# Expert blocks whose three layers are spread over three steps, with their weights in three transfers

## The chip, the cores and the metric

The kernel runs on one core of a Trainium2 chip. Its engines are TensorE (PE, with its weight loads as PEld), VectorE (DVE), ScalarE (ACT), GpSimd (POOL) and SyncE (SP); each takes its own instructions in order, and they meet by semaphores. The metric is the time of one execution in microseconds of device time. Before the change it is 2029.61 us, the median of three runs (2027.33 to 2029.68).

## The reference

The input is `x` (6250 nodes x 256, fp32) and 200,000 edges, `src` to `dst`, sorted by `dst`. Two stages follow each other:

```python
x = x + gnn(layernorm(x), edges)      # two layers
x = x + ffn(layernorm(x))             # six experts, two per node

# gnn, each of two layers l, over the edges and one loop per node:
h   = x @ W[l]
agg = segment_sum(norm[:, None] * h[src], dst) + b[l]
x   = relu(agg + x_res @ resW + resb)

# ffn:
rh     = relu(features @ router_w1 + router_b1)             # 256 -> 128
logits = softmax(rh @ router_w2 + router_b2)                # 6 experts
top_w, top_i = top_k(logits, 2); weights = softmax(top_w)
h1 = relu(features @ expert_w1 + b1)                        # 256 -> 256, each expert
h2 = relu(h1 @ expert_w2 + b2)
expert_out = h2 @ expert_w3 + b3
combined = sum over the two chosen experts of weight * expert_out
```

## The kernel before

The graph stages count the edges between tiles of nodes into matrices of fp16 and sum messages by products with them; they fill the time to about 1620 us and the change does not touch them. In the last pass each pair of node tiles (25 pairs, the last of one tile) is also normalised and routed: the router's products, the choice of two experts with their weights (`choices`, `gates`), and the place of each node in its expert's list (`place`), to which GpSimd scatters its row. There are two tables of such rows, one for the first choice and one for the second.

The **expert stage** reads these tables in blocks of 256 rows of one expert, at most 30 blocks for each choice (`NB`), so 60 blocks (`BLOCKS`). Blocks 0 to 29 compute the first choice's part and scatter `x + weight * expert` to a table `first_out`; blocks 30 to 59 compute the second choice's part, gather the rows of `first_out` by token, add to them and scatter to the output. Which expert and which row a block begins with stands in `block_table`. Its first 17 blocks (`EARLY_BLOCKS`) are settled early by `early_list`; the rest by `final_list` (lines 2215 to 2257), a chain of 25 small VectorE instructions, once the last tile has been placed.

The stage has no scheduler: each engine's order is written by hand, as a loop over steps b. TensorE's step was: the second layer of block b, the turn (four transposes) of block b+2, the first layer of block b+1, the output product of block b (`products`, lines 2130 to 2149).

```python
self.second_layer(pe, b, k)
self.turn(pe, b + 2, ...)
self.first_layer(pe, b + 1, ...)
self.outs(pe, b, k)
```

A layer writes two PSUM banks, one for each half of its 256 outputs. ScalarE empties the lower half with bias and relu (`low`, line 2158) and copies the turned rows (`y_copy`, line 2154); VectorE empties the upper half (`high`, line 2261). Per step VectorE also makes the scatter's row numbers (`index`, 2282 and 2284), the sum of bias and rows (`add_bias`, 2265), the normalised rows of block b+3 in the first choice (`normal`, 2289), and the result (`add_outs`, 2273). The last pair's routing is spread over the first steps by functions called `beside(b)`, on each engine.

SyncE loads weights and rows (`loads`, 2062 to 2077): after the result of block b it reads the expert from `block_table` (a `value_load`), loads the weights of block b+3 as one transfer into one of three slots (`load_weights`, 2042 to 2044), and then the rows of block b+6 (`load_rows`, 2047 to 2049). GpSimd scatters each block (2346) and, for the second choice, gathers the rows of block b+2 ahead of it (2339); the gather begins when all of the first choice has been stored.

## Time and profile before

| what | value |
|---|---|
| runs | 2027.33, 2029.61, 2029.68 us |
| profiled execution, span | 2027.2 us |
| expert stage, second layer of block 0 to outs of block 59 | 1622.15 to 2012.31 us |
| TensorE busy, whole span | 1845.7 us (91%) |
| VectorE, ScalarE, GpSimd busy | 1120.7, 771.5, 387.4 us |
| DMA, whole span | 208 GB/s of HBM traffic |
| weights | 60 transfers of 898.0 KB |
| rows | 60 transfers of 260.0 or 258.0 KB |

The page gives no other time of the profiled execution than its span, which lies 0.1 us below the fastest run and 2.4 us below the median. TensorE is busy for most of the span, but a stage can still wait: the busy share is an average over stages with different limits, and matmul ends are modelled. So the expert stage is read by itself, in stretches.

### The profile page before, as it was taken

The numbers are of one execution on the slowest core, as the hardware profiler recorded it, in microseconds if no ns is written. First come the engines' busy times: TensorE is split into PE (matmuls) and PEld (weight loads), VectorE is DVE, ScalarE is ACT, GpSimd is POOL, SyncE is SP. The second block draws the span as 40 slices with busy tenths as digits, with TensorE's granted clock in tenths as the row PEclk, the third lists the DMA queues.
The fourth block names the chain that finished last, engine by engine and source line by source line (L and its number), as shares of the span: only waits on it lengthen the run. The fifth ranks groups of instructions, "written<-read, shape, count | busy, mean of one in ns | idle before, by whom it ended". The sixth has DMA issues, their size and how long they took to land. (4 is left out here: it accounts for less than half of the span.)

```text
span 2027.2 us, 34554 instructions
## 1 busy us (share of the span) xinstructions
PE 1845.7 (91%) x11170; PEld 1128.0 (56%) x11170; DVE 1120.7 (55%) x2788; ACT 771.5 (38%) x1686; POOL 387.4 (19%) x403
## 2 busy tenths in 40 slices
PE   4448799999999999999959999999999988998886
PEld 3336555555555555555524445444454476886775
DVE  7246766666666666666504444444444566644443
ACT  2226755665566655665501222222222232221221
POOL 1680000000000000000000211111211133335664
PEclk8769899999999999999979999999999999998998
DMA  6255399998999972323364555444555556767783
GB/s 221 58 85 111 106 330 308 285 333 257 293 293 272 282 248 94 153 108 134 154 274 159 184 193 203 173 174 170 184 202 196 186 183 200 253 214 234 256 254 123
DMA packets 121920, 412.55 MB, mean 204 GB/s; under 512 B 14633, under 2 KB 75009, under 8 KB 115577
## 3 DMA queue, kind: packets, MB, share of 16 engines
q1 hardware_dynamic: 82936, 283.65, 40.2%
q0 software_dynamic: 37904, 124.85, 21.9%
q10 hardware_dynamic: 1008, 3.21, 0.4%
q8 instruction: 32, 0.52, 0.1%
q14 instruction: 40, 0.32, 0.1%
HBM read 201.60 MB, written 219.99 MB: 208 GB/s over the span
## 5 line engine op out<-in xcount | busy, mean ns | idle before, releaser
L1383 PE MATMUL bank<-parts,counts 128*128 128x512 f16 x2401 | 643.3, 378 | 0.0
L1383 PE MATMUL bank<-parts,counts_again 128*128 128x512 f16 x2401 | 540.3, 381 | 18.5 <-DMA counts_again<-counts_table 18.5
L1547 ACT ACTIVATE counts<-bank 128x392 f16<-128x392 f32 x800 | 395.1, 497 | 311.2 <-PE bank L1463 304.5
L1383 PEld LDWEIGHTS bank<-parts,counts_again 128*128 128x128 f16 x2401 | 234.1, 99 | 288.4 <-issue 17.0
L594 DVE TENSOR_TENSOR rows_lo<-pair_keys,iota_lo 128x2048 bf16<-128x2048 bf16 x200 | 244.9, 1225 | 239.4 <-PE bank L1463 239.3
L1463 PEld LDWEIGHTS bank<-rows_hi,rows_lo 128*128 128x128 bf16 x3200 | 227.6, 99 | 203.7 <-issue 27.1
L1463 PE MATMUL bank<-rows_hi,rows_lo 128*128 128x98 bf16 x3200 | 277.8, 210 | 11.3 <-DVE rows_hi L594 10.5
L1383 PEld LDWEIGHTS bank<-parts,counts 128*128 128x128 f16 x2401 | 192.5, 96 | 103.6 <-issue 1.1
L454 POOL DMA_INDIRECT first_rows<-route_rows,route_spot_i x49 | 47.9, 977 | 825.7 <-DVE tokens L445 817.7
L594 DVE TENSOR_TENSOR rows_hi<-pair_keys,iota_hi 128x1568 bf16<-128x1568 bf16 x200 | 193.5, 967 | 0.0
L2261 DVE TENSOR_SCALAR h_t<-bank,counts_again 128x256 f32<-128x256 f32 x120 | 57.7, 483 | 161.4 <-PE bank L2097 115.6
L2158 ACT ACTIVATE h_t<-bank,counts_again 128x256 f32<-128x256 f32 x120 | 56.9, 474 | 206.9 <-PE bank L2097 161.5
L2118 PE MATMUL bank<-counts_again,h_t 128*128 128x256 f32 x480 | 116.3, 386 | 10.5 <-issue 7.3
L2097 PE MATMUL bank<-h_t,counts_again 128*128 128x256 f32 x480 | 116.0, 385 | 9.7 <-DVE h_t L2261 5.7
L2097 PE MATMUL bank<-y_t,counts_again 128*128 128x256 f32 x480 | 116.8, 387 | 8.8 <-DMA counts_again<-expert_pack 5.0
L911 PE MATMUL bank<-both_w,feat 128*128 128x256 f32 x196 | 65.3, 465 | 60.8 <-issue 34.5
L1399 ACT ACTIVATE middle<-bank 128x256 f32<-128x256 f32 x98 | 37.3, 381 | 214.8 <-PE bank L1383 214.8
L2118 PEld LDWEIGHTS bank<-counts_again,h_t 128*128 128x128 f32 x480 | 92.2, 193 | 25.3 <-issue 11.6
L2097 PEld LDWEIGHTS bank<-h_t,counts_again 128*128 128x128 f32 x480 | 91.6, 193 | 25.0 <-ACT h_t L2158 9.3
L2097 PEld LDWEIGHTS bank<-y_t,counts_again 128*128 128x128 f32 x480 | 87.6, 192 | 22.2 <-DMA counts_again<-expert_pack 7.5
L375 DVE TENSOR_TENSOR route_prob<-bank,router_b_sb 128x12 f32<-128x12 f32 (+1 forms) x25 | 4.2, 170 | 162.4 <-PE bank L365 162.4
L183 PE MATMUL bank<-both_w,x_t 128*128 128x512 f32 x196 | 93.6, 600 | 0.5 <-ACT x_t L173 0.5
(259 smaller groups left out, 1843.1 us busy)
## 6 DMA issues: line engine op xcount, KB each, us to landing
counts_table<-counts SPq DMA_DIRECT2D x25, 3136.0 KB, 13.7
counts_again<-counts_table SPq DMA_DIRECT2D x24, 3136.0 KB, 11.4
counts_again<-expert_pack SPq DMA_DIRECT2D x60, 898.0 KB
first_rows<-zero_rows POOLq DMA_DIRECT2D x3, 10530.0 KB, 58.4
second_rows<-zero_rows POOLq DMA_DIRECT2D x3, 10449.0 KB, 70.2
res_tile<-res_table SPq DMA_DIRECT2D x98, 128.0 KB, 6.5
first_rows<-zero_rows POOLq DMA_DIRECT2D x1, 10270.0 KB, 61.8
second_rows<-zero_rows POOLq DMA_DIRECT2D x1, 10191.0 KB, 66.7
```

The costliest lines, as they stand in the source:

```text
L183: mm = nc.tensor.matmul(self.product_bank[:, :], self.x1_t[:, o, k * P:(k + 1) * P], self.both_w[:, self.l + 1, k, :], start=k == 0, stop= ...
L454: pool.indirect_dma_start(table, bass.IndirectOffsetOnAxis(ap=self.spot_i[:, b, c, o:o + 1], axis=0), rows[:, b, o, lo:hi], None, bounds_c ...
L594: return nc.vector.tensor_tensor(rows, k, v, ALU.is_equal)
L911: mm = nc.tensor.matmul(res_bank(t)[:, 0:dim], feat[:, t, k * P:(k + 1) * P], both_w[:, 0, k, dim:2 * dim], start=k == 0, stop=k == K2 - 1)
L1383: mm = nc.tensor.matmul(acc[:, 0:2 * dim], lhs, rhs, start=s == 0, stop=s == tiles)
L1399: nc.scalar.activation(middle[:, o, :], bank[half_bank + o][:, dim:2 * dim], ACT.Copy, scale=1.0 / LOW).then_inc(middle_out, 1)
L1463: mm = nc.tensor.matmul(bank[4 + q % 4][:, u * width:(u + 1) * width], rows_lo[:, r % 2, at, :, u % 2], rows_hi[:, r % 2, at, :, u % 2], s ...
L1547: nc.scalar.activation(counts[:, b, :, :].rearrange("p s (o n) -> p o s n", o=2)[:, :, :, q * QUAD:(q + 1) * QUAD], bank[4 + q % 4][:, 0:Q ...
L2097: mm = nc.tensor.matmul(to[m][:, 0:ROWS], weights_of(k, n)[:, kf, m * P:(m + 1) * P], source[:, k % 2, kf, :], start=kf == 0, stop=kf == K ...
L2118: mm = nc.tensor.matmul(outs_bank[k % 2][:, cols_of], h2_t[:, k % 2, kf, h * P:(h + 1) * P], weights_of(k, 2)[:, kf, :], start=kf == 0, st ...
L2158: nc.scalar.activation(to[:, k % 2, 0, :], frm[0][:, 0:ROWS], ACT.Relu, bias=bias_of(k, n, 0)).then_inc(low_out, 1)
L2261: nc.vector.tensor_scalar(to[:, k % 2, 1, :], frm[1][:, 0:ROWS], bias_of(k, n, 1), 0.0, ALU.add, ALU.max).then_inc(high_out, 1)
```

## The change

**The order.** A step on TensorE is now: the first layer of block b+2, the turn of block b+3, the second layer of block b+1, the output product of block b. Before the loop stand the first layer of block 1, the turn of block 2 and the second layer of block 0. ScalarE and VectorE follow in the same order. On VectorE the upper half of the first layer of b+2 comes first; then come the piece of routing or list, the row numbers, the bias sum, the normalised rows (now of block b+4), the upper half of the second layer of b+1, and the result. Each layer also waits until the halves of the block before it are emptied, since its bank is written while an older block is still on its way.

**The weights.** A block's weights are packed as three parts, each a layer's matrix with its bias (514, 514 and 768 columns), and loaded as three transfers with a semaphore each: a part is asked for as soon as its layer of the slot's former block has been emptied.

**The list.** `final_list` is cut into `blocks_held` (step 9), `final_list` (step 10) and `block_ends` (step 11). The routing pieces of the last pairs move by a step in places.

**A semaphore.** In `gather_sum`, five semaphores become one, `column_made`. That function belongs to the path for graphs that the counting path can't take.

```diff
+    W_AT = (0, K2 * dim + K2, 2 * (K2 * dim + K2), W_COLS)
...
-                def load_weights(self, sp, b, k):
-                    e = sp.value_load(block_table[0:1, 0, bass.ds(b, 1)], min_val=0, max_val=experts - 1)
-                    sp.dma_start(w[:, k % WB, :], expert_pack[bass.ds(e, 1), :, :].rearrange("a p n -> p (a n)")).then_inc(w_loaded[k % WB], 16)
+                def expert_of(self, sp, b):
+                    return sp.value_load(block_table[0:1, 0, bass.ds(b, 1)], min_val=0, max_val=experts - 1)
+
+                def load_weights(self, sp, e, k, n):
+                    part = slice(W_AT[n], W_AT[n + 1])
+                    sp.dma_start(w[:, k % WB, part], expert_pack[bass.ds(e, 1), :, part].rearrange("a p n -> p (a n)")).then_inc(w_loaded[n][k % WB], 16)
...
                 def early_weights(self, sp):
-                    for b in range(WB):
-                        self.load_weights(sp, b, b)
+                    for b, n in ((0, 0), (1, 0), (0, 1), (2, 0), (1, 1), (0, 2), (2, 1), (1, 2), (2, 2)):
+                        self.load_weights(sp, self.expert_of(sp, b), b, n)
+
+                def first_weights(self, sp, b, k):
+                    e = self.expert_of(sp, b + WB)
+                    sp.wait_ge(h1_low_out, b + 1)
+                    sp.wait_ge(h1_high_out, b + 1)
+                    self.load_weights(sp, e, k, 0)
...
                         def body(b, k):
+                            if not (isinstance(b, int) and b + 2 + WB >= BLOCKS):
+                                self.first_weights(sp, b + 2, k + 2)
+                            if not (isinstance(b, int) and b + 1 + WB >= BLOCKS):
+                                self.second_weights(sp, b + 1, k + 1)
...
+                            e = self.expert_of(sp, b + WB)
                             sp.wait_ge(result_ready, b + 1)
-                            self.load_weights(sp, b + WB, k)
+                            self.load_weights(sp, e, k, 2)
+                            if isinstance(b, int) and b + SB == EARLY_BLOCKS:
+                                sp.wait_ge(list_ready, 2)
+                                router.wait_scattered(sp, pairs)
                             if first is not None:
                                 self.load_rows(sp, b + SB, k, first)
...
                 def first_layer(self, pe, b, k, r):
-                    pe.wait_ge(w_loaded[k % WB], r * (16 * SB // WB) + 16 * (k // WB + 1))
+                    pe.wait_ge(w_loaded[0][k % WB], weights_count(r, k))
                     pe.wait_ge(y_out, b + 1)
+                    if not (isinstance(b, int) and b < 1):
+                        pe.wait_ge(h1_low_out, b)
+                        pe.wait_ge(h1_high_out, b)
...
                             b = r * SB + k
+                            if not (last and k + 2 >= SB):
+                                self.first_layer(pe, b + 2, *ahead(r, k, 2))
+                            if not (last and k + 3 >= SB):
+                                self.turn(pe, b + 3, *ahead(r, k, 3), second)
+                            if not (last and k + 1 >= SB):
+                                self.second_layer(pe, b + 1, *ahead(r, k, 1))
                             if isinstance(b, int) and b < 2 * SB:
                                 beside(b)
-                            self.second_layer(pe, b, k)
-                            if not (last and k + 2 >= SB):
-                                self.turn(pe, b + 2, (k + 2) % SB, r + (k + 2) // SB, second)
-                            if not (last and k + 1 >= SB):
-                                self.first_layer(pe, b + 1, (k + 1) % SB, r + (k + 1) // SB)
-                            self.outs(pe, b, k)
+                            self.outs(pe, b, k, r)
...
                             if c:
                                 dve.wait_ge(first_back[k % 3], (r - NB // SB) * (32 * SB // 3) + 32 * (k // 3 + 1))
-                            self.add_bias(dve, b, k, c)
+                            self.add_bias(dve, b, k, r, c)
+                            if not c and not (isinstance(b, int) and b + 4 >= NB):
+                                self.normal(dve, b + 4, k + 4, r + (k + 4) // SB)
+                            if not (last and k + 1 >= SB):
+                                second(b + 1, (k + 1) % SB)
                             if not (start and k < 2):
                                 dve.wait_ge(result_stored[k % 2], r * (16 * SB) + 32 * (k // 2))
-                            if not c and not (isinstance(b, int) and b + 3 >= NB):
-                                self.normal(dve, b + 3, k + 3, r + (k + 3) // SB)
                             self.add_outs(dve, b, k, c)
...
-                        if b == 8:
+                        if b == 7:
                             router.count_before(pe, LAST_PAIR, 1)
```

TensorE, before, from the second layer of block 0 on. `y_t` marks a first layer, `h_t` as second input a second layer, `ident` a turn, `counts_again,h_t` the outs (`counts_again` is the buffer that holds the weights); L415 and L416 count the router's choices.

```order
L2097 MATMUL bank<-h_t,counts_again 128x256 x4
L2091 MATMUL bank<-ident,rows 128x128 x4
L2097 MATMUL bank<-y_t,counts_again 128x256 x4
L2118 MATMUL bank<-counts_again,h_t 128x256 x4
L415 MATMUL bank<-route_pick,upper_b 128x24
L416 MATMUL bank<-route_pick,ones_b 128x24
L2097 MATMUL bank<-h_t,counts_again 128x256 x4
L2091 MATMUL bank<-ident,rows 128x128 x4
L2097 MATMUL bank<-y_t,counts_again 128x256 x4
L2118 MATMUL bank<-counts_again,h_t 128x256 x4
L2097 MATMUL bank<-h_t,counts_again 128x256 x4
```

In each step the two layers stand on either side of the turn, and the outs follow the first layer.

The same engine now, from the second layer of block 0 on.

```order
L2126 MATMUL bank<-h_t,counts_again 128x256 x4
L2126 MATMUL bank<-y_t,counts_again 128x256 x4
L2120 MATMUL bank<-ident,rows 128x128 x4
L2126 MATMUL bank<-h_t,counts_again 128x256 x4
L2155 MATMUL bank<-counts_again,h_t 128x256 x4
L2126 MATMUL bank<-y_t,counts_again 128x256 x4
L2120 MATMUL bank<-ident,rows 128x128 x4
L2126 MATMUL bank<-h_t,counts_again 128x256 x4
L415 MATMUL bank<-route_pick,upper_b 128x24
L416 MATMUL bank<-route_pick,ones_b 128x24
L2155 MATMUL bank<-counts_again,h_t 128x256 x4
```

First layer, turn, second layer and outs now belong to four different blocks, and the count of choices stands between a second layer and the outs of the block before.

VectorE, before, at the end of the list in step 9 (L2251 to L2257) and the rest of that step.

```order
L2251 TENSOR_TENSOR more_held<-placed_to 128x2x5
L2252 TENSOR_SCALAR more_held<-placed_to 128x2
L2253 TENSOR_TENSOR weighed<-past,more_held 128x360
L2254 TENSOR_REDUCE block_end<-weighed 128x60
L2256 TENSOR_TENSOR block_end<-block_end,placed_to 128x60
L2257 TENSOR_TENSOR ends<-block_end,block_row 128x43
L2282 TENSOR_SCALAR unused<-row_of,ends 128x2
L2284 TENSOR_TENSOR to_token<-rows,unused 128x2
L2265 SCALAR_TENSOR_TENSOR both_w<-counts_again,rows 128x256 x2
L2289 TENSOR_SCALAR rows<-rows 128x256 x2
L2273 SCALAR_TENSOR_TENSOR both_w<-bank,rows,both_w 128x256 x2
L2261 TENSOR_SCALAR h_t<-bank,counts_again 128x256 x2
```

Both upper halves (`h_t`) stand together, after the result (L2273), and the list stands ahead of all of the step's other work.

The same engine now, in step 11, from the upper half of the first layer of block 13 on, with the last part of the list (L2310 to L2316).

```order
L2320 TENSOR_SCALAR h_t<-bank,counts_again 128x256
L2310 TENSOR_TENSOR more_held<-placed_to 128x2x5
L2311 TENSOR_SCALAR more_held<-placed_to 128x2
L2312 TENSOR_TENSOR weighed<-past,more_held 128x360
L2313 TENSOR_REDUCE block_end<-weighed 128x60
L2315 TENSOR_TENSOR block_end<-block_end,placed_to 128x60
L2316 TENSOR_TENSOR ends<-block_end,block_row 128x43
L2342 TENSOR_SCALAR unused<-row_of,ends 128x2
L2344 TENSOR_TENSOR to_token<-rows,unused 128x2
L2325 SCALAR_TENSOR_TENSOR both_w<-counts_again,rows 128x256 x2
L2349 TENSOR_SCALAR rows<-rows 128x256 x2
L2320 TENSOR_SCALAR h_t<-bank,counts_again 128x256
```

The two upper halves are apart: the second layer's comes after the bias sum (L2325) and the normalised rows (L2349), and the result after it.

## Rows read from the trace of the kernel before

**Rows 1.** Stretches of the expert stage: us, busy us per engine (instructions), TensorE clock, DMA.

```profile
1622.15:1704.20 82.05, 67.23 (x319) 56.44 (x320) 55.28 (x200) 21.39 (x43) 25.61 (x26) 0.96 0.58 181
1704.20:1818.08 113.88, 113.05 (x561) 99.10 (x560) 67.59 (x193) 30.91 (x60) 38.88 (x40) 1.00 0.75 243
1818.08:1830.73 12.65, 7.39 (x30) 5.95 (x29) 3.63 (x10) 1.54 (x3) 7.54 (x8) 0.80 0.36 110
1830.73:1939.43 108.70, 95.34 (x450) 80.18 (x449) 45.97 (x125) 24.41 (x48) 66.74 (x65) 0.98 0.78 251
1939.43:1996.81 57.38, 52.28 (x251) 44.67 (x252) 27.40 (x76) 13.91 (x27) 36.73 (x36) 1.00 0.79 252
1996.81:2012.31 15.50, 14.87 (x70) 12.47 (x68) 8.02 (x20) 2.97 (x6) 10.14 (x10) 1.00 0.24 83
```

**Rows 2.** Timeline, TensorE, one step: start, us, line, out<-in, count [idle before <-releaser].

```profile
1760.74 1.89 PE L2097 MATMUL bank<-h_t,counts_again 128*128 128x256 f32 x8
...
1762.47 0.60 PE L2091 MATMUL bank<-ident,rows 128*128 128x128 f32 x4
...
1762.91 1.89 PE L2097 MATMUL bank<-y_t,counts_again 128*128 128x256 f32 x8
...
1764.63 1.89 PE L2118 MATMUL bank<-counts_again,h_t 128*128 128x256 f32 x8
...
1766.36 1.89 PE L2097 MATMUL bank<-h_t,counts_again 128*128 128x256 f32 x8
```

**Rows 3.** Waits of TensorE, 1622 to 1704 us: total, times, longest.

```profile
PE bank L2091 <- DVE rows L2289: 9.7, 3, 6.4
PE bank L415 <- DVEq L403: 3.4, 2, 1.8
```

**Rows 4.** Timeline, VectorE: first and last of the 25 list instructions.

```profile
1688.95 0.16 DVE L2229 TENSOR_TENSOR held_i<-placed_to,region_base 128x12 int32<-128x12 f32 x1
...
1696.20 0.20 DVE L2257 TENSOR_TENSOR ends<-block_end,block_row 128x43 f32<-128x43 f32 x1
```

**Rows 5.** The chain of work that ended last: start, us, what.

```profile
1935.09 7.46 DMA counts_again<-expert_pack
```

**Rows 6.** Timeline, all engines, around the turn to the second choice.

```profile
1812.98 0.88 DVE L2273 SCALAR_TENSOR_TENSOR both_w<-bank,rows,both_w 128x256 f32<-128x256 f32 x2 [0.22 <-PE bank L2118]
...
1814.68 0.33 SPq L2044 DMA_DIRECT2D counts_again<-expert_pack  x1
...
1821.05 1.07 POOL L2339 DMA_INDIRECT rows<-first_out,to_token  x1 [4.09 <-issue]
...
1825.27 0.88 DVE L2265 SCALAR_TENSOR_TENSOR both_w<-counts_again,rows 128x256 f32<-128x256 f32 x2 [7.68 <-DMA rows<-first_out,to_token]
...
1827.61 3.75 PE L2118 MATMUL bank<-counts_again,h_t 128*128 128x256 f32 x8 [5.26 <-issue]
```

**Rows 7.** Timeline, VectorE and TensorE, a step of the second choice.

```profile
1908.09 1.89 PE L2097 MATMUL bank<-y_t,counts_again 128*128 128x256 f32 x8
...
1912.93 0.48 DVE L2261 TENSOR_SCALAR h_t<-bank,counts_again 128x256 f32<-128x256 f32 x1 [4.49 <-remote]
...
1913.56 1.97 PE L2097 MATMUL bank<-h_t,counts_again 128*128 128x256 f32 x8 [1.85 <-DVE h_t L2261]
```

**Rows 8.** Timeline, SyncE: three weight loads issued in a row.

```profile
1612.01 2.54 SPq L2044 DMA_DIRECT2D counts_again<-expert_pack  x3
```

**Rows 9.** Timeline, SyncE: weights and rows of two steps of the second choice.

```profile
1929.94 0.04 SPq L2044 DMA_DIRECT2D counts_again<-expert_pack  x1
1931.41 0.00 SPq L2049 DMA_DIRECT2D rows<-second_rows  x1
1935.09 0.03 SPq L2044 DMA_DIRECT2D counts_again<-expert_pack  x1
1937.96 0.02 SPq L2049 DMA_DIRECT2D rows<-second_rows  x1
```

**Rows 10.** Groups by line, GpSimd, 1830.73 to 1996.81 us: busy, mean ns, idle before.

```profile
L2346 POOL DMA_INDIRECT out_dram<-both_w,to_token x51 | 52.3, 1026 | 16.6 <-issue 15.4 <-DVE to_token L2284 1.2
```

More of the change, by code:

```diff
@@ L1912, in _ @@
                     work.early_list(dve)
+                    work.blocks_held(dve)
                     work.final_list(dve)
+                    work.block_ends(dve)
                     work.first_normal(dve)
@@ L1995, in expert_blocks @@
             list_ready = sem("list_ready")
-            w_loaded = [sem(f"w_loaded{b}") for b in range(WB)]
+            w_loaded = [[sem(f"w{n}_loaded{b}") for b in range(WB)] for n in range(3)]
             rows_loaded = [sem(f"rows_loaded{b}") for b in range(SB)]
@@ L2068, in after @@
                         return body
+                    for b in range(2):
+                        self.first_weights(sp, b, b)
+                    self.second_weights(sp, 0, 0)
                     for b in range(2 * SB):
-                        if b + SB == EARLY_BLOCKS:
-                            sp.wait_ge(list_ready, 2)
-                            router.wait_scattered(sp, pairs)
                         after(True)(b, b)
@@ L2075, in loads @@
                     rounds(sp, NB - SB, BLOCKS - SB, after(False))
-                    for b in range(BLOCKS - SB, BLOCKS - WB):
+                    for b in range(BLOCKS - SB, BLOCKS):
                         after(None)(b, b)
@@ L2167, in low_halves, with first, second @@
                 def low_halves(self, act, beside):
+                    def first(b, k):
+                        self.low(act, b, k, 0, h1_bank, h1_t, h1_ready, h1_low_out)
+                    def second(b, k):
+                        self.low(act, b, k, 1, h2_bank, h2_t, h2_ready, h2_low_out)
                     def steps(r, last=False):
@@ L2170, in steps @@
                             b = r * SB + k
-                            self.low(act, b, k, 1, h2_bank, h2_t, h2_ready, h2_low_out)
                             if not (last and k + 2 >= SB):
-                                self.y_copy(act, b + 2, (k + 2) % SB)
+                                first(b + 2, (k + 2) % SB)
+                            if not (last and k + 3 >= SB):
+                                self.y_copy(act, b + 3, (k + 3) % SB)
                             if not (last and k + 1 >= SB):
-                                self.low(act, b + 1, (k + 1) % SB, 0, h1_bank, h1_t, h1_ready, h1_low_out)
+                                second(b + 1, (k + 1) % SB)
                             if isinstance(b, int) and b < 2 * SB:
                                 beside(b)
+                    first(1, 1)
+                    self.y_copy(act, 2, 2)
+                    second(0, 0)
                     steps(0)
@@ L2302, in high_halves, with first, second @@
                 def high_halves(self, dve, beside):
+                    def first(b, k):
+                        self.high(dve, b, k, 0, h1_bank, h1_t, h1_ready, h1_high_out)
+                    def second(b, k):
+                        self.high(dve, b, k, 1, h2_bank, h2_t, h2_ready, h2_high_out)
                     def steps(r, c, start=False, last=False):
@@ L2305, in steps @@
                             b = r * SB + k
-                            self.high(dve, b, k, 1, h2_bank, h2_t, h2_ready, h2_high_out)
-                            if not (last and k + 1 >= SB):
-                                self.high(dve, b + 1, (k + 1) % SB, 0, h1_bank, h1_t, h1_ready, h1_high_out)
+                            if not (last and k + 2 >= SB):
+                                first(b + 2, (k + 2) % SB)
                             if isinstance(b, int) and b < 2 * SB:
```

135 lines of the change are left out of this document (81 added, 54 removed).

## The prediction

> **What bounds the kernel now.** I read the table of stretches first. It cuts the expert stage, from the second layer of block 0 to the last product of block 59, into six pieces of 390.16 us together [rows 1]. A step of the block loop is 28 TensorE instructions (4 transposes and three times 8 matmuls), so the counts in that table give the steps: 11, 20, 1, 16, 9, and the last three blocks. Next the timeline of TensorE in the second piece: second layer, turn, first layer and output product follow each other without a gap, 1.73, 0.44, 1.72 and 1.73 us from start to start, and the next step begins after 5.62 us [rows 2]. That is the floor of a step, and I set each piece against it:
>
> - A, blocks 0 to 11: 82.05 against 11 x 5.62 = 61.8, 20.2 over.
> - B, to 31: 113.88 against 112.4, 1.5 over.
> - C, one step, from the first expert choice to the second: 12.65, 7.0 over.
> - D, 32 to 48: 108.70 against 89.9, 18.8 over.
> - E, to 57: 57.38 against 50.6, 6.8 over.
> - F, the end: 15.50 against 14.4 (5.62, then 5.18 without a turn, then 3.46 and a drain), 1.1 over.
>
> The sum is 55.4 us in which TensorE stands still or runs below its full clock. What ends those waits differs by piece. In A it is VectorE: the normalised rows came late (9.7 us in three waits), and the choices that a router product counts came late (3.4) [rows 3]. The longest of the first kind is the block list: its instructions run in one row on VectorE from 1688.95 to 1696.20 [rows 4], in front of the rows that the next turn needs. In E the first layer waits for its weights; the chain of waits has a transfer of 7.46 us there [rows 5]. In C, VectorE waits for the rows gathered from the first choice's result, and everything behind it waits too [rows 6]. In D the signals of TensorE reach the other engines late: the first layer that begins at 1908.09 takes 1.89, yet VectorE, idle for 4.49 us, empties its upper half only at 1912.93, 3.0 us after its end, and TensorE then stands 1.85 us [rows 7]. I see no cause for this lateness in the trace, only its size.
>
> **The change part by part.** *The order on TensorE.* No product is added or dropped; a step stays 5.62. What moves is the time between a layer and its reader. Before, the second layer's halves had the turn and the next first layer as cover (0.44 + 1.72 = 2.2 us), the first layer's halves one output product (1.73). Now outs of b+1 follow second layer b+1 after outs of b, first layer b+3, turn b+4 and second layer b+2: 1.73 + 1.72 + 0.44 + 1.73 = 5.6 us. The first layer's halves have 0.44 + 1.73 + 1.73 + 1.72 + 0.44 = 6.1. The turn's copy loses: it had 5.6 and has the second layer and outs, 3.5. The added waits of both layers for the empty bank look back a whole step, and what is queued behind them on TensorE would not run sooner without them.
>
> In A this covers VectorE's long stretches, but not all. VectorE's own work in a step of the first choice is about 3.5 us, so a router piece of up to 2 us fits into the step, and one of 3.4 to 3.8 overruns. I place three overruns: step 2, where gates, placing and variance come together; step 10, where the middle third of the list stands (about half of the 7.3 us in [rows 4]). By adding up VectorE's row the rows for the next turn come 0.9 us late each time. In step 7 the count of choices now stands on TensorE ahead of the same step's outs, 3.9 us into the step, while the choices end about 5.9 us into it: 2.0. With the router's own dozen products (about 1.0) A keeps 0.9 + 0.9 + 2.0 + 1.0 = 4.8 and gives back 15.4.
>
> *Weights in thirds.* Before, a transfer was asked for after the result of block b, 1.9 us after its outs (the sum from 1812.98 on, the load at 1814.68 [rows 6]), and wanted 7.8 us after them (a step, a second layer and a turn): 5.9 us, against 7.46 in the slow case. Now each third is asked for when its own layer is emptied, three steps before the slot is used again: 3 x 5.62 - 1.73 - 2.0 = 13.1 us (the 2.0 taken like that 1.9) for the first layer. B's 1.5 and E's 6.8 go, if SyncE keeps up. Four transfers a step in place of two, each with a read of the list: three weight loads issued back to back cost (2.54 - 0.33) / 2 = 1.10 us apiece [rows 8], so 4.4 of 5.62. In the second half the pitch was 1.47 and once 2.87 [rows 9]. At 1.47 a step takes 5.9 on SyncE, 0.3 too much, and 25 steps use up 6.5 us of lead, about what there is to spare (13.1 - 7.46). So I take no cost, and hold 2.87 as the far end.
>
> The Trainium skill, DMA: Bandwidth & Descriptors, section "Rules for kernel authors", speaks against this part: many small transfers should be coalesced. Its section on one DMA's anatomy fits 2.0 us plus bytes by 436 GB/s, which makes 4.1 us of one whole block and 2.6 + 2.6 + 2.9 = 8.1 of three parts; one behind another, with 2.6 for the rows, a step would take 10.7 us. The trace disagrees with "one behind another": in B a step already carries a whole block, its rows and two scatters, 6.7 us by the fit without the scatters, in 5.69 at a DMA share of 0.75 [rows 1].
>
> *The rest.* The pack of weights is written by as many transfers as before, and the one semaphore in place of five belongs to the gathering path, which has no row in this trace: nothing for both. The list in three pieces is inside A's sum. Its middle third is now ready in step 10 in place of 9; the first reader is the row load in SyncE's body 11, after the result of block 11, more than 3 us later: nothing.
>
> *The turn to the second choice* stays. Block 29's result is done at 1812.98 + 0.88, the gather starts at 1821.05 and VectorE goes on at 1825.27 [rows 6], 12.4 us after outs of 29 ended (about 1812.8). Before, TensorE had a step, a second layer, a turn and a first layer to do in that time, 9.5 us. Now it has step 30, first layer 33 and a turn, 5.62 + 1.72 + 0.44 = 7.8; second layer 32 waits for the upper half of second layer 31, which VectorE takes after the bias sum on the gathered rows, at about 12.4 + 0.9 + 0.4 = 13.7. It stands 5.9 where it stood 5.26, so C becomes about 0.6 worse.
>
> *D.* A lateness of 3.0 us fits into 5.6 and 6.1, so the waits on the layers' halves go; into the turn's 3.5, less about 1 us for the copy itself, it does not. Also GpSimd issues four indirect transfers a step here, at 1.03 us and a gap of 15.4 / 51 = 0.3 [rows 10], 5.3 of 5.62: it has next to no rest, and I can't exclude that the lateness grows with that. Bounds for D and E together: nothing left of 25.6 over, or all of it. I take 10 left, 0.4 us a step, nearer to the good end, since the cover of both layers exceeds the lateness in [rows 7].
>
> Sum: A 15.4, B 1.5, C -0.6, D and E 15.6, F 0.8 (outs of 59 no longer waits) = 32.7 us. The profiled execution's span is 2027.2; the runs have a median of 2029.61, 2.4 above it, which I carry along: 2029.6 - 32.7 = **1997 us**.
>
> **The rivals.**
>
> 1. *All is absorbed*: D and E at 5.62. For it: cover above the lateness. Against: the turn's shorter cover. 10 us more, 1987.
> 2. *The second half doesn't move*: what sets its pace is GpSimd and the DMA engines (share 0.78 in D and 0.79 in E [rows 1]), and late signals come whenever these are full; a faster TensorE only meets them sooner. For it: 5.3 of 5.62 on GpSimd. Against: in the same rows neither is full at 6.8 us a step. 15.6 less, 2013.
> 3. *VectorE becomes the bound of A*: half of A's gain goes, 2005. Against: [rows 1], 55.28 busy of 82.05.
> 4. *SyncE's queue*, the other side: with four issues a step it decides the pace of D and E from the point at which a step costs more than the whole gain elsewhere: 166.1 + 17.1 = 183.2 for 25 steps, plus the spare lead of 5.6, is 7.55 a step, 1.9 us an issue. Halfway between 1.47 and 2.87, at 2.17, it would be 8.7 x 25 - 5.6 = 212 us, 46 more than now less 17 gained: 2058. For it: single rows at 2.87. Against: 1.10 where GpSimd is quiet. The page's sum above (10.7 us in all 60 steps, some 300 us more) is the far case of this rival; the trace bears it out so little that it has one of the hundred chances here.
>
> **How the numbers follow.** Forecast 0.48, rival 1 0.19, rival 2 0.20, rival 3 0.07, rival 4 0.06. The range runs from rival 1 with a little more given back at the start (1985) to just beyond rival 2 (2016); rival 4 and the rest are left out. A measurement of this kernel tells a change of about 0.2%, 4 us. Slower is rival 4, 0.05 of its 0.06; the remaining 0.01 and 0.02 of rival 2 give 0.03 for no change; faster 0.92.
>
> **What would show it.** Right: no wait of TensorE for VectorE's halves or for weights worth more than 2 us together after block 32; steps of 5.62 from block 12 to 29; about 2 us of waiting for the choices near step 7; a stand of 5 to 6 us at the second layer of block 32. If waits on the turn's copy appear in D, the 0.4 us a step are there. Wrong: first layers waiting for a third of their weights while SyncE issues without rest (rival 4), GpSimd without gaps and steps above 6.3 us (rival 2), or A above 70 us (rival 3).

## The result, and the profile after

The changed kernel takes 2011.28 us (median of 4 runs, 2009.25 to 2014.58) against 2029.64. The measured ratio is 0.9924, interval 0.9908 to 0.9941; the two medians divided give 0.9910. The forecast was 1997. So 18 us were gained by the medians, 15 by the ratio, where 33 were forecast. The profiled execution has a span of 2006.8 (time 2009.25, the lowest of the four).

To compare stretches I cut both traces at the same places, where the weight load of a block's output product starts on TensorE:

```
us between the output products of blocks  0-11   11-30  30-32  32-48   48-57  57-59
before                                    82.16  108.26 19.45  108.41  56.49  9.60
after                                     67.63  106.76 18.91  106.65  60.16  6.26
gained                                    14.5   1.5    0.5    1.8     -3.7   3.3
forecast (pieces A, B, C, D and E, F)     15.4   1.5    -0.6   15.6 (D, E)    0.8
```

So the miss has one place. In the second choice's blocks (32 to 57) 15.6 us were to come back, and 166.81 stand where 164.90 stood. The 3.3 at the end is the deeper order and no gain: two layers more, 3.46 us, now lie ahead of output product 0. The start of the stage lies elsewhere in each execution (output product 0 between 1622 and 1632 us in the kernels below, none of them changed ahead of it but for the layout of the weights), so I don't divide the 18 us finer than this.

The table of stretches after the change, with the columns of [rows 1]:

```profile
1622.20:1689.83 67.63, 64.37 (x322) 55.17 (x320) 52.50 (x192) 20.88 (x42) 26.06 (x27) 1.00 0.75 232
1689.83:1796.59 106.76, 106.76 (x533) 94.06 (x532) 66.24 (x188) 29.32 (x58) 40.41 (x40) 1.00 0.84 251
1796.59:1815.50 18.91, 13.65 (x57) 11.43 (x56) 5.62 (x16) 2.34 (x6) 11.13 (x12) 0.82 0.51 150
1815.50:1922.15 106.65, 94.59 (x450) 79.66 (x448) 47.04 (x131) 24.24 (x50) 66.34 (x65) 0.98 0.82 245
1922.15:1982.31 60.16, 52.96 (x249) 44.96 (x248) 23.46 (x65) 11.96 (x26) 37.20 (x36) 0.97 0.77 238
```

The second line is a TensorE without a gap, 19 steps of 5.62. In the fourth it is busy 94.59 of 106.65, hardly better than the 95.34 of 108.70 in [rows 1]. The main waits of that half, the last two lines of the table, from the same trace (1815.5 to 1982.3 us; total, times, longest):

```profile
DVE h_t L2320 <- remote: 31.3, 7, 6.0
ACT h_t L2202 <- remote: 29.5, 8, 6.1
PEld bank L2120 <- DMA rows<-second_rows: 16.2, 12, 3.6
PE bank L2120 <- DMA rows<-second_rows: 11.3, 11, 3.2
ACT y_t L2198 <- remote: 14.6, 3, 5.3
PE bank L2126 <- issue: 5.3, 4, 1.6
PE bank L2126 <- DVE h_t L2320: 2.2, 1, 2.2
PE bank L2126 <- ACT h_t L2202: 0.5, 1, 0.5
```

Two things are to be seen. No wait of TensorE is for weights any more, but twelve of its weight loads wait for a block's rows. And VectorE and ScalarE wait for something "remote" up to 6 us: their input is long done, but the signal isn't there.

These waits add up to what is missing. The half takes 166.81 us where its floor is 140.04, 26.8 more. In about 19 of them TensorE stands still: 11.3 for rows, 3.9 in three first layers that begin when the turn's copy is done, and 4.0 in three waits for a layer's halves. The other 7.5 are products that take longer: TensorE is busy 94.59 + 52.96 = 147.55 us, and its granted clock reads 0.98 and 0.97.

What goes on during a late signal shows when GpSimd's row stands beside it:

```profile
1828.79 1.11 POOL L2416 DMA_INDIRECT out_dram<-both_w,to_token  x1 [3.37 <-DVE both_w L2333]
...
1831.51 1.04 POOL L2409 DMA_INDIRECT rows<-first_out,to_token  x1 [0.30 <-issue]
...
1832.94 1.89 PE L2126 MATMUL bank<-h_t,counts_again 128*128 128x256 f32 x8
...
1838.15 1.03 POOL L2409 DMA_INDIRECT rows<-first_out,to_token  x1 [0.30 <-issue]
1840.27 0.48 DVE L2320 TENSOR_SCALAR h_t<-bank,counts_again 128x256 f32<-128x256 f32 x1 [5.95 <-remote]
1840.42 0.47 ACT L2202 ACTIVATE h_t<-bank,counts_again 128x256 f32<-128x256 f32 x1 [3.24 <-remote]
...
1840.90 3.41 PE L2126 MATMUL bank<-h_t,counts_again 128*128 128x256 f32 x8 [2.18 <-DVE h_t L2320]
```

From 1828.79 to 1839.18 GpSimd runs eight indirect transfers in a row, 0.3 us apart (a chain, from here on). The second layer that starts at 1832.94 is over at 1834.83; VectorE takes its upper half only at 1840.27, 5.4 us later and about 1 us after the chain ended. TensorE has its next second layer to do by then, which writes the same bank, and stands 2.18 us until that bank is empty. Most of the late signals of this half come within 1.3 us after the end of a chain, the others while its last transfers run (up to 3.2 us before its end). The same stands in the trace of before, at the place of [rows 7], where I had written that I saw no cause. GpSimd's row there, first and last of eight in a chain that ends at 1911.84:

```profile
1901.31 1.04 POOL L2339 DMA_INDIRECT rows<-first_out,to_token  x1 [2.85 <-DVE to_token L2284]
...
1910.84 1.00 POOL L2346 DMA_INDIRECT out_dram<-both_w,to_token  x1 [0.30 <-issue]
```

VectorE went on at 1912.93. That the two go together could have been read from the trace of before, on a row that I had only added up; that one causes the other takes the runs below. Nor is 3.0 us the longest case there. In the same trace a second layer is over at 1859.96, VectorE takes its upper half 4.7 us later, and TensorE stands 3.20:

```profile
1858.07 1.89 PE L2097 MATMUL bank<-h_t,counts_again 128*128 128x256 f32 x8
...
1864.63 0.87 DVE L2261 TENSOR_SCALAR h_t<-bank,counts_again 128x256 f32<-128x256 f32 x2 [4.72 <-remote]
...
1865.35 2.65 PE L2118 MATMUL bank<-counts_again,h_t 128*128 128x256 f32 x8 [3.20 <-DVE h_t L2261]
```

SyncE, which issues weights and rows, falls behind in the same stretch:

```profile
1933.47 5.09 SPq L2051 DMA_DIRECT2D counts_again<-expert_pack  x3
1939.99 0.00 SPq L2056 DMA_DIRECT2D rows<-second_rows  x1
...
1943.18 0.70 PE L2120 MATMUL bank<-ident,rows 128*128 128x128 f32 x4 [3.22 <-DMA rows<-second_rows]
```

Three issues take 5.09 where [rows 8] has 2.54; the rows are asked for at 1939.99, and TensorE has waited 3.22 us for them when they land.

### The profile page after: what moved, and what is told of

It reads as the page before. It is cut to its first block and busy times, and to the rows that moved or that the text cites. A ratio compares the mean times of both kernels' runs of the same rounds, so it can differ in the third digit from the quotient of the medians.

```text
span 2006.8 us, 35596 instructions
## 1 busy us (share of the span) xinstructions
PE 1843.3 (92%) x11170; PEld 1127.9 (56%) x11170; DVE 1121.0 (56%) x2788; ACT 769.0 (38%) x1686; POOL 391.2 (19%) x403
## 6 DMA issues: line engine op xcount, KB each, us to landing
counts_table<-counts SPq DMA_DIRECT2D x25, 3136.0 KB, 10.7
counts_again<-counts_table SPq DMA_DIRECT2D x24, 3136.0 KB, 11.3
```

## The experiments

Three theories went in. **G**: GpSimd's indirect transfers hold up the other engines' signals and SyncE. **S**: SyncE's four issues a step are the bound. **W**: the DMA engines are full. The table gives each run's median, its ratio to the kernel before on the same chip, and, from one profiled execution each, the same stretches as above (before 82.16, 108.26, 19.45, 108.41, 56.49; the floor of the last two is 89.91 and 50.13). The kernel before has medians of 2028 to 2034 on these chips, so times of different runs are best compared by their ratios.

```
                    median  ratio (interval)         0-11   11-30   30-32  32-48   48-57
split_only          2030.39 0.9998 (0.9982, 1.0014)  86.12  106.76  18.62  105.80  58.00
fewer_reads         2006.16 0.9892 (0.9865, 0.9919)  67.56  106.76  18.26  103.73  60.96
rows_first          2012.11 0.9914 (0.9886, 0.9941)  67.53  106.76  18.93  108.27  57.92
small_weights       2021.71 0.9942 (0.9923, 0.9960)  67.80  106.76  18.49  106.35  66.74
no_gather           1977.82 0.9749 (0.9714, 0.9783)  67.60  106.76  11.24   89.91  50.13
half_gather         1982.36 0.9753 (0.9729, 0.9777)  67.68  106.76  16.49   89.91  50.13
before_no_gather    2004.13 0.9860 (0.9836, 0.9884)  84.07  108.13  11.24   89.91  50.57
busy_instead        1984.44 0.9773 (0.9733, 0.9813)  68.41  106.76  11.95   89.91  50.13
busy_longer         1981.64 0.9765 (0.9735, 0.9794)  67.54  106.76  13.22   89.91  50.13
busy_full           1982.98 0.9754 (0.9706, 0.9802)  67.57  106.76  15.97   89.91  50.13
one_list            2024.60 0.9962 (0.9941, 0.9983)  73.69  106.76  18.60  108.77  64.11
scatter_add         1980.30 0.9739 (0.9720, 0.9757)  67.87  106.76  11.24   89.91  50.13
best                1980.18 0.9755 (0.9724, 0.9787)  66.88  106.76  11.24   89.91  50.13
before_scatter_add  2006.22 0.9887 (0.9854, 0.9920)  82.59  108.18  11.24   93.36  51.87
```

**split_only**, the weights in three transfers alone: the kernel before with the layout, the loads and the waits of the change, but its own order of products.

```diff
+                            if not (isinstance(b, int) and b + 1 + WB >= BLOCKS):
+                                self.first_weights(sp, b + 1, k + 1)
+                            self.second_weights(sp, b, k)
...
-                            self.load_weights(sp, b + WB, k)
+                            self.load_weights(sp, e, k, 2)
```

> The kernel before with the weights in three transfers alone: old order of products, list in one piece. In the changed kernel the second half (from the output product of block 32 to that of block 57) takes 166.8 us, as before (164.9). Theory G (GpSimd's indirect transfers hold up SyncE's instructions and the other engines' signals): the first twelve blocks stay at 82 us, the second half stays at 165 or gets some us longer since SyncE now has four issues in a step; about 2025 us, the gain being the earlier start and the weights that came late in the first half. Theory S (the SyncE queue's own length bounds the second half): the same or worse, 2025 to 2035. Theory W (the DMA engines' bandwidth): 2020 to 2025. If instead the order on TensorE were worth nothing, this kernel alone would reach 2011.

Measured: no gain. 11 to 30 comes down to the floor, since no weights are late; 0 to 11 is 4 us longer where no change was expected (TensorE's weight loads wait 11.2 us for normalised rows, 6.8 at once; the cause of the longer stretch stays open). So the 14.5 us of the first piece belong to the order and the list.

**fewer_reads**, SyncE reads a block's expert once where it can, and keeps it for the later steps of the same six.

```diff
-                    e = self.expert_of(sp, b + WB)
+                    e = self.expert_of(sp, b + WB, k + WB)
```

> The changed kernel, but SyncE reads a block's expert once for its three transfers where it can (8 reads in 6 steps in place of 18). Changed kernel: a step of SyncE takes 6.6 us in the second half, and TensorE waits 11.3 us (its weight loads 16.2) for rows of the second choice. Theory S: a step of SyncE falls below 5.6, all waits for rows go, second half 166.8 to 147, 1991 us. Theory G: the waits for rows go, the late signals stay: second half about 153, 1998 us. Theory W: nothing changes, 2011.

The waits for rows are gone, as both S and G had it, and the time is not: 164.69 in the second half against 166.81, where G had 153 and S 147. In place of the rows TensorE waits for ScalarE's copy of the turn, and the trace shows the sharpest case of a late signal (GpSimd's chain of twelve ends at 1858.98; its first and last row, and what lies beside it):

```profile
PEld bank L2137 <- ACT y_t L2209: 15.7, 8, 5.8
```
```profile
1843.00 1.25 POOL L2427 DMA_INDIRECT out_dram<-both_w,to_token  x1 [2.99 <-DVE both_w L2344]
...
1850.06 0.60 PE L2131 MATMUL bank<-ident,rows 128*128 128x128 f32 x4
...
1857.95 1.03 POOL L2420 DMA_INDIRECT rows<-first_out,to_token  x1 [0.31 <-issue]
1858.89 0.60 ACT L2209 ACTIVATE y_t<-bank 128x512 f32<-128x512 f32 x1 [6.64 <-remote]
1859.55 3.78 PE L2137 MATMUL bank<-y_t,counts_again 128*128 128x256 f32 x8 [5.43 <-ACT y_t L2209]
```

The transposes are over at 1850.66. ScalarE, idle, copies them 8.2 us later, in the moment the chain ends. S falls: with SyncE relieved, the pace hardly changes. G's figure was missed too: the late signals took the place of the waits for rows, so the two can't be counted one by one.

**rows_first**, the rows ahead of the weights in SyncE's order.

```diff
+                                sp.wait_ge(result_ready, b + 1)
...
+                                self.load_rows(sp, b + SB, k, first)
+                                self.load_weights(sp, self.expert_of(sp, b + WB), k, 2)
                             if not (isinstance(b, int) and b + 2 + WB >= BLOCKS):
                                 self.first_weights(sp, b + 2, k + 2)
```

> The changed kernel, but SyncE asks for a block's rows and its last third of weights as soon as a result is there, ahead of the other two thirds. Theory S and theory G (SyncE issues too slowly for its step): the waits for rows go, but the backlog moves to the weights: TensorE waits for weights in place of rows, second half 160 to 167, 2005 to 2011 us. If it was only the place in the queue and not the rate: second half 152, 1997 us. Theory W: 2011.

As S and G had it: the waits move to the weights (14.0 us in 11), the time stays.

```profile
PE bank L2129 <- DMA counts_again<-expert_pack: 14.0, 11, 2.4
```

**small_weights**, few bytes in as many transfers.

```diff
-                    part = slice(W_AT[n], W_AT[n + 1])
+                    part = slice(W_AT[n], W_AT[n] + 64 if few else W_AT[n + 1])
```

> The changed kernel, but in the second half each third of weights moves only its first 64 columns (the products then use weights of an earlier block): as many transfers and reads by SyncE, a fraction of the bytes. Theory W (DMA bandwidth): the second half falls from 166.8 to 150 or less, about 1994 us. Theory G (GpSimd's four indirect transfers a step hold up signals and SyncE): it stays above 158, 2003 to 2011 us, with waits for signals or rows still there.

W falls. The stretch from 32 to 48 has a DMA share of 0.46 (second figure from the end) and 125 GB/s in place of 0.82 and 245, and takes 106.35. The late signals are still there, and blocks 48 to 57 take 66.74, so that the time is longer than expected:

```profile
1825.21:1931.56 106.35, 93.71 (x450) 79.90 (x449) 47.17 (x133) 23.65 (x49) 66.17 (x63) 0.98 0.46 125
```

**no_gather**, **half_gather**, **before_no_gather**: two, three and two indirect transfers a step in place of four.

```diff
-                    for h in range(2):
-                        pool.indirect_dma_start(rows[:, k % SB, h, X2], None, first_out, ...)
```

> The changed kernel without the gather of the first choice's results in the second half (the results of the first choice are then missing from the output): GpSimd issues two indirect transfers a step in place of four. Theory G: SyncE's step falls to 5.6 or less, late signals and waits for rows go, second half 166.8 to 142..148, and the turn to the second choice loses its wait of some 6 us: about 1983 us. Theory S (SyncE has the same four issues): the second half stays at 160 or more, about 2000 us. Theory W: one of about seven megabytes in ten steps less to move, second half 155 to 160.

> The changed kernel, but only one half of a block's rows is gathered in the second half of the stage (the other half lacks the first choice's result): three indirect transfers a step on GpSimd, 3 x 1.33 = 4.0 us of 5.62. Without the gather a step took 5.62, with it 6.7. Theory G in the form that a signal waits for a pause of GpSimd: pauses of 1.6 us in each step are enough, second half 142 to 148, about 1985 us. Theory G in the form that each transfer costs the same: half of the excess is left, second half 154, 1995 us.

> The kernel before without the gather in the second half. Theory G: with the late signals gone the old order on TensorE has no wait of that kind either; what is left in the second half is the weights that land late: from 164.9 to 142..150, and the turn to the second choice loses its 7 us: about 2000 us. If the order's cover mattered in the second half also without late signals, it stays at 153 or more, 2010 us.

In the two without a gather VectorE's wait for it is gone too; half_gather keeps it. All three stand at the floor in the second half (50.57 is nine steps of 5.62, the floor of the old order), with not one wait of TensorE from block 32 to the end in the first two. The stretch from 32 to 48 in half_gather:

```profile
1822.96:1912.86 89.90, 89.90 (x449) 79.20 (x448) 47.50 (x128) 24.69 (x49) 48.89 (x48) 1.00 0.86 271
```

It is no matter of degree: three transfers a step cost nothing, four cost 26.8 us. SyncE has the same four issues a step there, so S falls again. And the old order does as well as the new one (140.48): without late signals it has nothing to give in this half.

**busy_instead**, **busy_longer**, **busy_full**: plain instructions of GpSimd in place of the gathers (2, 16, 26 iotas a step).

```diff
-                        pool.indirect_dma_start(rows[:, k % SB, h, X2], None, first_out, ...)
+                        for n in range(13):
+                            ins = nc.gpsimd.iota(rows[:, k % SB, h, X2][:, 19 * n:19 * n + 19], [[1, 19]], 0, 0, ...)
```

> The changed kernel, but where the two gathers of a step stood GpSimd runs two plain instructions of about the same length (an iota of 176 columns into the same rows; the first choice's results are then missing), so that it is as busy as before and issues two indirect transfers a step. If the signals and SyncE are held up by indirect transfers alone, the second half takes 140 to 143 us as without the gather, about 1980 us. If they are late because GpSimd has no pause, whatever it does, it takes 155 or more, 2000 us.

> As the run with two plain instructions in place of the gather, which turned out to take 0.54 us a step and not 2.1: now sixteen iotas of 32 columns a step (about 2.7 us if each takes the 0.17 of the small iotas at the program's start), so that GpSimd is busy some 5.3 us of 5.62 as with four indirect transfers. If the late signals come from indirect transfers alone, the second half takes 140 to 143 us, about 1980 us. If they come from GpSimd having no pause, 155 or more, 2000 us; GpSimd itself as the bound would show as TensorE waiting in every step.

> Twenty-six iotas a step in place of the gather. With sixteen (1.73 us) GpSimd was busy 4.0 of 5.62 us, no more than with three indirect transfers, and every step took 5.62. Now 2.8 us of iotas and 2.6 of transfers with their gaps, 5.4 of 5.62: as full as with four indirect transfers. If the lateness belongs to the indirect transfers, a step stays at 5.62 and the second half at 140 to 143, 1981 us; if it comes from a GpSimd without a pause, 155 or more, 2000 us.

The first two were too short to tell anything (0.54 and 1.73 us of iotas a step). The third does: GpSimd's row has no rest above 0.5 us, and the steps from block 32 to 57 take the floor.

```profile
1854.43 0.98 POOL L2417 DMA_INDIRECT out_dram<-both_w,to_token  x1 [0.17 <-issue]
1855.72 0.99 POOL L2417 DMA_INDIRECT out_dram<-both_w,to_token  x1 [0.31 <-issue]
1856.71 2.85 POOL L2410 IOTA rows<- 128x19 f32 x26
1859.72 0.99 POOL L2417 DMA_INDIRECT out_dram<-both_w,to_token  x1 [0.17 <-issue]
```
```profile
1816.38:1906.29 89.91, 89.91 (x450) 79.22 (x449) 48.24 (x128) 24.70 (x49) 79.90 (x455) 1.00 0.84 255
```

GpSimd is busy 79.90 us of 89.91, more than in the changed kernel (66.34 of 106.65), at the same DMA share. So it is not a busy GpSimd, but the four indirect transfers a step. All runs that help take away a gather, so the gathers alone could be meant; a chain of eight scatters in the first twelve blocks, with signals as late, speaks against that (the rows stand in the next section). Whether the number or the missing pause does it is less clear; the next section has a stretch with four transfers a step and a pause after each four.

**one_list**, the changed kernel with the list in one piece.

```diff
                             work.blocks_held(dve)
-                        if b == 10:
                             work.final_list(dve)
-                        if b == 11:
                             work.block_ends(dve)
```

> The changed kernel with the block list in one piece in step 9. By the prediction's reckoning VectorE's own work of a step is 3.5 us, the list 7.3: the step overruns by 5.2, the rows for the next turn come that much late, and the first twelve blocks take 67.6 + 3 to 5 = 71 to 73 us. If the new order's cover alone did it and the pieces nothing, they stay at 68.

73.69, 6.1 us more, 0.7 above the expected range: the reckoning of 5.2 of overrun holds about (one wait for the rows of the next turn is 4.47), and the cover alone would not have done it. That the second half is 6 us longer too lies in its spread: in the kernels here with four transfers a step it takes 164 to 173.

```profile
1690.80 0.93 PE L2118 MATMUL bank<-ident,rows 128*128 128x128 f32 x4 [4.47 <-DVE rows L2347]
```

**scatter_add**, **before_scatter_add**, **best**: nothing is gathered; the first choice goes straight into the output, the second is added there by the transfer.

```diff
-    pool.indirect_dma_start(table, bass.IndirectOffsetOnAxis(ap=to_token[:, k % SB, h:h + 1], axis=0), result[:, k % 2, cols_of], None,
-                            bounds_check=nodes - 1, oob_is_err=False).then_inc(result_stored[k % 2], 16)
+    pool.indirect_dma_start(out, bass.IndirectOffsetOnAxis(ap=to_token[:, k % SB, h:h + 1], axis=0), result[:, k % 2, cols_of], None,
+                            bounds_check=nodes - 1, oob_is_err=False, compute_op=op).then_inc(result_stored[k % 2], 16)
```

> The changed kernel, but the first choice's results are scattered into the output, and the second choice's are scattered with an addition there, so that nothing is gathered: two indirect transfers a step in both halves. Theory G: as without the gather, second half 140 to 142, no wait at the turn to the second choice, 1978 us, plus what a transfer with an addition costs more (not shown by any run here). If such a transfer takes GpSimd or the DMA engines twice as long, the pace is that of four transfers again: second half 160 to 167, about 2000 us.

> The kernel before with the scattered addition alone. Theory G: second half 140.5 as without the gather, no wait at the turn to the second choice: 2004 to 2008 us, so that the change on TensorE is worth 25 us more once GpSimd issues two transfers a step (1980.3). If the transfers with an addition (1.54 us in place of 1.03) hold up the old order, which has less cover: second half 145 to 155, 2010 to 2020 us.

> The kernel with the scattered addition, and the count of the last pair's choices moved behind the output product of block 7, at the head of step 8. The count waited 1.8 us for VectorE there (weight load's row): the first twelve blocks fall from 67.9 to about 66, the rest is as with the scattered addition alone (1980.3 us): 1978 us. If VectorE's next pieces, which read the count, then come late in step 8, the gain is given back: 1980.

The scattered addition computes all of the reference, and its 1980.3 us beat both kernels. A transfer with an addition takes GpSimd 1.54 us in place of 1.03 and the DMA engines are busier (share 1.02 against 0.82), with no wait:

```profile
L2414 POOL DMA_INDIRECT out_dram<-both_w,to_token x32 | 49.3, 1542 | 40.6 <-DVE both_w L2336 30.8 <-issue 9.8
```
```profile
1816.04:1905.94 89.90, 89.90 (x449) 79.21 (x448) 45.50 (x128) 24.69 (x49) 49.35 (x32) 1.00 1.02 256
```

On the kernel before, the addition leaves 5.2 us over the new order's floor in the second half, where the weights come in one transfer; TensorE's weight loads wait 2.9 us for them:

```profile
PEld bank L2097 <- DMA counts_again<-expert_pack: 2.9, 5, 0.9
```

Against that kernel the change is worth 26 us by the medians in place of 18 (by the ratios 30 in place of 15). Moving the count (best) takes 1.0 us from the first piece, which the time does not show: its wait is gone, waits for rows are longer.

## Why the prediction was wrong

- **The first twelve blocks: right in the main.** 14.5 of 15.4. The count was waited for in step 7 as forecast, 1.8 us where 2.0 stood; the waits for rows were smaller than 0.9 twice (1.5 in three). Not forecast were 1.9 us in step 5, so part of the agreement is luck. It is the second half's mechanism again: the last pair's four scatters join with four others in a chain that ends at 1649.81, all of them scatters. ScalarE copies a turn that was over at 1644.36 only 4.0 us later, 1.4 us before the chain's end, and VectorE takes the upper half of a layer that was over at 1646.09 only 1.5 us after that end.

```profile
1639.78 0.97 POOL L2416 DMA_INDIRECT first_out<-both_w,to_token  x1 [5.59 <-DVE both_w L2333]
...
1648.39 0.60 ACT L2198 ACTIVATE y_t<-bank 128x512 f32<-128x512 f32 x1 [4.82 <-remote]
1648.84 0.97 POOL L2416 DMA_INDIRECT first_out<-both_w,to_token  x1 [0.30 <-issue]
1649.09 1.97 PE L2126 MATMUL bank<-y_t,counts_again 128*128 128x256 f32 x8 [0.82 <-issue]
...
1651.31 0.48 DVE L2320 TENSOR_SCALAR h_t<-bank,counts_again 128x256 f32<-128x256 f32 x1 [4.26 <-remote]
```

- **Blocks 11 to 30: right**, at the floor, 5.62 a step at a share of 0.84. With SyncE's four transfers a step this is far from the 10.7 us that the prediction kept as the far case of rival 4. The Trainium skill, DMA: Bandwidth & Descriptors, section "Anatomy of one DMA — SWDGE (gpsimd) path", states the fit behind that sum for transfers that GpSimd issues, and these are SyncE's. The rule in its section "Rules for kernel authors", to coalesce many small transfers, speaks of mostly overhead under 64 KB; the three parts here are 257, 257 and 384 KB, so the trace does not bear on it.
- **The turn to the second choice: right in mechanism.** The second layer of block 32 stands 5.26 us, where 5.9 was forecast, as VectorE waits for gathered rows. The piece came out 0.5 us better and not 0.6 worse:

```profile
1804.69 0.88 DVE L2325 SCALAR_TENSOR_TENSOR both_w<-counts_again,rows 128x256 f32<-128x256 f32 x2 [9.03 <-DMA rows<-first_out,to_token]
...
1806.12 3.75 PE L2126 MATMUL bank<-h_t,counts_again 128*128 128x256 f32 x8 [5.26 <-issue]
```

- **The second half: wrong.** 15.6 us were to come back, and 1.9 were lost. The step that failed is "a lateness of 3.0 us fits into 5.6 and 6.1, so the waits on the layers' halves go". Both sides of it were off. I took the lateness from one row as a number that stays; it was 4.7 us in another row of before, 5.4 here and 8.2 in fewer_reads. And the cover, the time between a layer and what needs its halves, was not 5.6 and 6.1: each layer also waits for its emptied bank, so a layer's halves must be out when the same layer of the next block begins, 5.62 - 1.73 = 3.9 us after its own end. The prediction holds that nothing would run sooner without this wait; at 1840.90 TensorE stands 2.18 us in it.

  What the runs show in place of a fixed lateness is its cause: with four indirect transfers a step the half takes 26.8 us above the floor, with three or two nothing. By the rows, four transfers take 4 x (1.03 + 0.3) = 5.3 us, so a TensorE that needs 5.62 for a step leaves hardly a pause between them (an estimate from [rows 10]). Chains of eight stand in both kernels, one of twelve in fewer_reads. They end when GpSimd waits for VectorE's next result (3.37 us ahead of the chain that begins at 1828.79), that is, when TensorE has stood. That more cover would only put this off is argued from these rows; no run shows it by itself.

  The trace of before has the counterpart. In blocks 48 to 57 its first layers waited for weights, as the prediction says of E, and a step took 56.49 / 9 = 6.28 us. There a pause of 1.1 to 2.2 us mostly follows GpSimd's four transfers of a step, and from 1944.2 to 2000.7 us no engine waits for a late signal. The change took the waits for weights away, the chains of eight came in, and the piece went from 56.49 to 60.16. A pause is no full protection: in small_weights a chain of four with 0.92 us of pause ahead of it (1877.07 to 1882.14) goes with a signal 3.8 us late. GpSimd's waits in that stretch of before (total, times, longest):

```profile
POOL rows L2339 <- DVE to_token L2284: 10.3, 7, 2.2
```

  Rival 2, at 0.20, had the mechanism in its words ("late signals come whenever these are full; a faster TensorE only meets them sooner"). Its sum, 2013, is 2 us from the measured time, and its sign, steps above 6.3 us, came: 6.67 from 32 to 48. Of the two causes that it names, the DMA engines fell with small_weights. What I held against it, that neither is full at 6.8 us a step, did not count, as I read the rows: the pauses are what the late signals cost.
- **SyncE: a term that was put at nothing.** "So I take no cost" for four issues a step failed as well. They fell behind, and TensorE stood 11.3 us for rows, more than for anything else in that half. The spare lead of the prediction, 13.1 - 7.46, was that of the first layer's weights; the rows, which stand last in a step of SyncE, were not counted. Yet it is no cause of its own: with the waits for rows away (fewer_reads) that half was 2 us shorter, within its spread, the signals being late as well, and with three indirect transfers a step (half_gather) the same four issues left no wait.
- **The list in pieces: right**, 6.1 us in one_list.

## What to carry to other kernels

When an engine starts long after its input was ready and the profile names a "remote" releaser, lay GpSimd's row beside it: a chain of indirect transfers that ends at about that time was the cause here, and the deeper order on the other engines did not cover it. Count the indirect transfers a step against the step you are aiming at, not the one you have: at 6.7 us four looked as if they had room, at 5.62 they had none. Taking transfers away (an addition in the scatter in place of a gather, once all earlier writes have landed) was worth more here than the whole reordering (23 us on the kernel before, by the ratio, against 15).

## What the runs showed of the hardware

- Signals from TensorE reached ScalarE and VectorE up to 8.2 us late while GpSimd ran indirect transfers 0.3 us apart, mostly about when the chain ended. With plain instructions in place of half of them (busy_full), none was late. What path they share is not shown by any run.
- SyncE's three issues took 5.09 us in such a stretch, against 2.54 in [rows 8].
- Three indirect transfers a step (GpSimd busy 48.89 of 89.90 us) left no late signal and steps of 5.62; four cost 26.8 us in 25 steps. Four in steps of 6.28 us (before, blocks 48 to 57) left none late either.
- An indirect transfer with an addition took 1.54 us on GpSimd against 1.03 without; the share of the DMA engines read 1.02 and nothing waited for them.
